# Two stages of mixture-of-experts behind graph attention: routing by chunks, slot lists from one-hot products, experts that gather their rows

## The chip, the cores and the metric

One Trainium2 chip, of which the program uses one core. The metric is the device time of one execution in microseconds (us), the median over the runs.

## The reference

A graph with N = 6250 nodes of D = 256 float32 features and E = 206250 edges goes through two layers. Each is graph attention and then a mixture of experts, both added to the residual:

```python
x = x + _L0_gnn_ref(_layernorm(x), ..., edge_attr_3, edge_index)
x = x + _L0_ffn_ref(_layernorm(x)[None], ...)[0]
x = x + _L1_gnn_ref(_layernorm(x), edge_index, ...)
x = x + _L1_ffn_ref(_layernorm(x)[None], ...)[0]
```

The two mixtures have 8 experts with 1024 hidden units. Layer 0's sends each token to its two best experts; before the experts it normalises its input a second time, with a scale and shift of each expert:

```python
probs = softmax(xt @ Wr + br); top_p, top_idx = top_k(probs, 2)
weights = top_p / top_p.sum(-1)
xn = (xt - mu) * rsqrt(var + 1e-5);  xe = xn * ln_g[e] + ln_b[e]
y = gelu(xe @ W1[e] + b1[e]) @ W2[e] + b2[e]
out = sum of weights * y over the two
```

Layer 1's sends each token to its best expert, drops what is over an expert's capacity (977 tokens), uses relu, multiplies by the probability, and replaces what is not finite.

## The kernel before

`build` (L1777) runs its stages one after the other, each with its own buffers and semaphores; between two stages all engines meet. They are: a plan of the edges; then for each layer a node stage (projections), an edge stage (attention, with rows gathered by GpSimd), and `ffn_phases` (L1216), which is a routing stage and an expert stage. The change is in `ffn_phases` and in one scratch tensor of `scratch`.

**Routing.** The tokens are NT = 49 tiles of 128, taken as 7 chunks of R = 7. SyncE loads a chunk's residual rows `r_xs` and attention sums `r_ag`, two chunks ahead, and stores the combined rows (`keep_rows`, L1289). VectorE combines each chunk (L1424 to L1436): it divides the sums by the denominators, seven multiplies of a tile each, every one waiting for the last (`done`), adds bias and residual, and takes the statistics. Only after the last chunk come mean and variance of all tiles (`stats`), the normalisation of 49 tiles (L1455), in layer 0 the statistics of the normalised rows (L1462) and a second normalisation (L1473). In one loop VectorE copies a tile to `r_xg` (L1468), TensorE transposes it (L1363), ScalarE copies it out (L1396) and TensorE multiplies it by the router's weights (L1369). Then VectorE works out softmax, choices, and by two matmuls (L1382, L1383) the place of each token among those of its expert. Experts' slots are laid out in blocks of TB = 256. SyncE has filled `sc_xb` with zeros meanwhile (L1312). GpSimd scatters each tile's rows, 258 numbers with token number and weight behind the features, to their slots in `sc_xb`: 49 indirect DMAs for the first choice (L1341), in layer 0 49 more for the second (L1347), each chunk of these behind VectorE's exchange of the weight in the row (L1560).

**Experts.** A loop over pairs of blocks, two buffers. SyncE's queue, for each block: its rows `x_xin` from `sc_xb` (L1606), in layer 0 scale and shift (L1608, L1609), both weight matrices of 1 MB, both biases (L1610 to L1613), all of them once VectorE has taken the outputs of the block before the last. TensorE: 16 fp32 matmuls into `x_ps_h` (L1676), the next block's four transposes (`turn`, L1661), 16 matmuls into `x_ps_y` (L1687). ScalarE applies the activation. VectorE makes `x_xT` of the next block (L1707 or L1710), adds the bias (L1738), weighs (L1744, L1748), in layer 1 bounds the values (L1752 to L1757) and adds the residual (L1761), and works out row numbers and weights of the next block from the last two columns of its rows (L1715 to L1720, `rows_of`). GpSimd's queue, in its order: in layer 1 two gathers of residual rows `x_xr` (L1641) as soon as those numbers are there; once the block is added, two scatters, in layer 0 accumulating (L1646), in layer 1 plain (L1649); a wait until they have landed. `hold` is a wait on a semaphore against a value of the loop.

## Time and profile before

| | |
|---|---|
| median of 3 runs | 6622.04 us (6620.52 to 6622.79) |
| the profiled execution | 6616.8 us |
| its span on the core | 6614.6 us |
| busy: TensorE, VectorE, ScalarE, GpSimd | 69%, 53%, 21%, 55% |
| granted TensorE clock, mean | 0.87 of 2.4 GHz |
| layer 0's routing stage | about 2474 to 2828 us |
| layer 0's expert stage | about 2828 to 3676 us |
| layer 1's routing stage | about 5897 to 6158 us |
| layer 1's expert stage | about 6158 us to the end |

Every stage is visible in the page's second part, which cuts the span into 40 slices. A record of TensorE is a half of an fp32 matmul. PE is TensorE, PEld its weight loads, DVE VectorE, ACT ScalarE, POOL GpSimd, SP SyncE; SPq and POOLq are DMA issues or the sequencer. A bracket behind a row tells how long the engine had been idle and what released it.

### The profile page before, as it was taken

Reading aid. Unit: us, or ns where it says so; the run is one execution under the profiler, and the core shown is the slowest. Engines: PE = TensorE matmul, PEld = TensorE weight load, DVE = VectorE, ACT = ScalarE, POOL = GpSimd, SP = SyncE. Lnnn points to the kernel's source line nnn. Section 1 sums busy time; section 2 is a strip of 40 time slices with the busy share of each in tenths; the row PEclk is TensorE's granted clock in tenths of the full one; section 3 lists DMA queues with packets and bytes.
Section 4 is the critical chain, followed back from the end, with each engine's and each line's share of the span. In section 5 each row is a group of like instructions: output and inputs, shape, how many; then the busy total and the mean of one; then the engine's idle time right before and its main releaser. Section 6 shows DMA issues by size and latency. Waiting matters only on the chain. (4 is left out here: it accounts for less than half of the span.)

```text
span 6614.6 us, 94515 instructions
## 1 busy us (share of the span) xinstructions
PE 4549.3 (69%) x18923; PEld 3390.2 (51%) x18923; DVE 3515.0 (53%) x6341; ACT 1391.7 (21%) x2978; POOL 3661.8 (55%) x3707
## 2 busy tenths in 40 slices
PE   1578888888888872189999435665656565643698
PEld 0345555555545552179999424444444444433698
DVE  5678787887878857111111334444444453544244
ACT  1333333333333320022222201111111111101122
POOL 1577777777777730512222177777777777711322
PEclk9899999999999995589999768888888888875899
DMA  7555555555555525255556555555555555532455
GB/s 215 176 164 162 159 165 157 165 161 158 162 159 162 160 74 211 74 169 184 184 184 184 137 137 138 142 137 142 138 141 139 140 141 138 141 108 110 171 199 187
DMA packets 717825, 1021.19 MB, mean 154 GB/s; under 512 B 301952, under 2 KB 531459, under 8 KB 692504
## 3 DMA queue, kind: packets, MB, share of 16 engines
q0 software_dynamic: 183456, 485.95, 27.8%
q1 hardware_dynamic: 488947, 491.67, 23.9%
q10 hardware_dynamic: 45188, 41.42, 2.0%
q14 instruction: 205, 1.67, 0.1%
q8 instruction: 29, 0.48, 0.0%
HBM read 868.25 MB, written 152.93 MB: 154 GB/s over the span
## 5 line engine op out<-in xcount | busy, mean ns | idle before, releaser
L767 POOL DMA_INDIRECT e_rows<-sc_table,e_eidx x3224 | 3164.9, 982 | 1019.4 <-issue 952.4
L872 PE MATMUL e_ps_o<-e_rows,e_oh 128*128 128x264 f32 x6448 | 1687.5, 407 | 154.6 <-ACT e_res L957 134.0
L872 PEld LDWEIGHTS e_ps_o<-e_rows,e_oh 128*128 128x128 f32 x6448 | 1211.5, 198 | 568.0 <-issue 389.9
L1132 DVE TENSOR_TENSOR e_rows<-e_rows,e_ps_w 128x1024 f32<-128x1024 f32 x806 | 970.4, 1207 | 11.0 <-ACT e_rows L953 10.9
L957 ACT COPY e_res<-e_ps_o 32x264 f32<-32x264 f32 x806 | 296.2, 368 | 1938.9 <-PE e_ps_o L876 1378.5
L844 PE MATMUL e_ps_X<-e_ident,e_alog 128*104 128x128 f32 x496 | 112.4, 399 | 811.5 <-ACT e_alog L937 811.5
L1062 DVE SCALAR_TENSOR_TENSOR e_u<-e_encr,e_adst,e_ps_hd 128x512 f32<-128x512 f32 x806 | 580.5, 739 | 162.9 <-ACT e_encr L933 106.5
L1676 PE MATMUL x_ps_h<-x_xT,x_w 128*128 128x256 f32 x2624 | 645.8, 404 | 14.8 <-DMA x_b<-in_L_ffn_b_dram 14.8
L1676 PEld LDWEIGHTS x_ps_h<-x_xT,x_w 128*128 128x128 f32 x2624 | 637.3, 337 | 18.8 <-issue 15.6
L1687 PE MATMUL x_ps_y<-x_w,x_hT 128*128 128x256 f32 x2624 | 579.9, 379 | 0.0
L933 ACT ACTIVATE e_encr<-e_ps_enc 128x512 f32<-128x512 f32 x806 | 477.3, 592 | 437.1 <-PE e_ps_enc L804 433.8
L1646 POOL DMA_INDIRECT sc_x<-x_y,x_idx x108 | 167.9, 1554 | 664.7 <-DVE x_idx L1720 648.1
L1687 PEld LDWEIGHTS x_ps_y<-x_w,x_hT 128*128 128x128 f32 x2624 | 492.9, 190 | 63.5
L844 PEld LDWEIGHTS e_ps_X<-e_ident,e_alog 128*104 128x104 f32 x496 | 95.1, 264 | 838.2 <-issue 838.2
L1085 DVE TENSOR_TENSOR e_ps_k<-e_ps_X,e_y 104x512 f32<-104x512 f32 x31 | 21.7, 699 | 845.5 <-ACT e_y L941 845.5
L1699 ACT ACTIVATE x_hT<-x_ps_h,x_b 128x256 f32<-128x256 f32 x656 | 305.1, 474 | 779.1 <-PE x_ps_h L1676 778.8
L876 PE MATMUL e_ps_o<-e_res,e_sel 128*128 128x264 f32 x1488 | 455.6, 388 | 0.0
L815 PE MATMUL e_ps_X<-e_u,e_hwide 128*104 128x512 f32 x806 | 416.2, 597 | 50.9 <-DVE e_u L1065 50.9
L804 PE MATMUL e_ps_enc<-e_at,e_w_enc 96*128 96x512 bf16 x806 | 309.2, 384 | 200.3 <-DVE e_u L1062 111.3
L1053 DVE TENSOR_SCALAR e_ohT<-e_at,e_nid 96x512 bf16<-96x512 int16 x806 | 295.3, 367 | 280.2 <-PE e_ps_X L820 210.8
L804 PEld LDWEIGHTS e_ps_enc<-e_at,e_w_enc 96*128 96x128 bf16 x806 | 78.0, 97 | 515.3 <-issue 506.6
L1341 POOL DMA_INDIRECT sc_xb<-r_xt,r_slot_i x98 | 94.7, 967 | 437.8 <-DVEq L1546 408.5
(291 smaller groups left out, 4402.3 us busy)
## 6 DMA issues: line engine op xcount, KB each, us to landing
x_w<-in_L_ffn_W_dram SPq DMA_DIRECT2D x112, 1024.0 KB
e_at<-sc_grp SPq DMA_DIRECT2D x403, 192.0 KB
x_w<-in_L_ffn_w_dram SPq DMA_DIRECT2D x60, 1024.0 KB
e_rows<-sc_table,e_eidx POOLq DMA_INDIRECT x3224
e_at<-sc_grp SPq DMA_DIRECT2D x403, 96.0 KB
sc_agg<-e_res ACTq DMA_DIRECT2D x806, 33.0 KB
...
```

What stands on the lines that cost most here:

```text
L767: pool.indirect_dma_start(rows[:, k, s, j, :], None, dr["table"][:, :], bass.IndirectOffsetOnAxis(eidx[:, k, s, j:j + 1], 0)).then_inc(s_r ...
L804: nc.tensor.matmul(ps_enc[:, :], w_enc[:, h * P:(h + 1) * P], at[:, ring(s), 0, :].bitcast(BF16), start=True, stop=True).then_inc(s_enc, 1)
L815: nc.tensor.matmul(ps_X[0:COLS, :], hwide[:, 0, COLS - HEADS * (s + 1):2 * COLS - HEADS * (s + 1)], u[:, par(s), 0, :], start=(s == 0), st ...
L872: nc.tensor.matmul(ps_o[:, 0:ROW], oh[:, k, at_j:at_j + P], rows[:, k, s, j, :], start=(j == 0), stop=False)
L876: nc.tensor.matmul(ps_o[:, 0:ROW], sel[:, k, s * WIN:s * WIN + P], seen, start=False, stop=True).then_inc(s_o, 1)
L933: nc.scalar.activation(encr[:, h, :], ps_enc[:, :], ACT.Relu).then_inc(s_relu, 1)
L957: nc.scalar.copy(res[0:WIN, kept(s), :], ps_o[0:WIN, 0:ROW]).then_inc(s_ev, 1)
L1062: nc.vector.scalar_tensor_tensor(u[:, p, h, :], encr[:, h, :], adst[:, h:h + 1], ps_hd[:, h, :], ALU.add, ALU.mult).then_inc(s_u, 1)
L1132: nc.vector.tensor_tensor(part, part, ps_w[:, k, :, s * HEADS:(s + 1) * HEADS].unsqueeze(3).to_broadcast([P, CH, HEADS, DH]), ALU.mult).th ...
L1676: mm = nc.tensor.matmul(ps_h[:, j % 4, 0:TB], w1[:, k, c, :].rearrange("p (m j) -> p j m", j=FC)[:, j, :], xT[:, k, c, :], start=(c == 0), ...
L1687: mm = nc.tensor.matmul(ps_y[:, s, 0:D], hT[:, k, j, s * P:(s + 1) * P], w2[:, k, j, :], start=(j == 0), stop=(j == FC - 1))
L1699: nc.scalar.activation(hT[:, k, j, :], ps_h[:, j % 4, 0:TB], ACT.Gelu if first else ACT.Relu, bias=b1[:, k, j:j + 1]).then_inc(s_act, 1)
```

## The change

In the routing stage, mean and variance of a chunk are worked out as soon as it is combined. ScalarE normalises it from scale and bias per row (`even`), which in layer 0 is the double normalisation at once; the logits are multiplied by the second standard deviation afterwards. TensorE transposes these rows directly, tile by tile, without the copy. SyncE stores the normalised rows in token order in `xn`, and the tokens' weights behind them, 2 numbers each. No rows are scattered and nothing is filled with zeros. Instead a list of slots is made: with a slot's number as 128 * hi + lo, VectorE makes for each tile and choice a one-hot row of lo (128 columns) and one of hi times a mark (120 columns in layer 0, 72 in layer 1), and TensorE's products of the two add up to a table of which token (and which choice) lies in each slot. In the expert stage GpSimd gathers a block's rows from `xn` by that list, while the block two before is in work; SyncE no longer loads rows, and issues the first weight matrix first. In layer 0 the weight of a row is chosen from its two by the list.

The diff, cut (new buffers, semaphores and GpSimd's constants left out):

```diff
+    def even_rows(c):
+        sp.wait_ge(s_xtn, (c + 1) * R)
+        sp.dma_start(xn[c * R * P:(c + 1) * R * P, 0:D].rearrange("(t p) d -> p t d", p=P),
+                     xt[:, c * R:(c + 1) * R, :]).then_inc(s_rows, 16)
...
+        if c >= 4:
+            even_rows(c - 4)
     for c in range(R - 2, R):
         sp.wait_ge(s_agu, c + 1)
         keep_rows(c)
     sp.dma_start(rows_in[NP:NP + TB, :].rearrange("(p s) d -> p (s d)", p=P), zero[:, 0:SUB * D]).then_inc(s_kept, 16)
-    sp.wait_ge(s_fill, 16 * -(-n_slot // (8 * P)))
-    sp.sem_inc(s_in, 1)
+    sp.dma_start(xn[NP:NP + TB, :].rearrange("(p s) d -> p (s d)", p=P), zero[:, :]).then_inc(s_rows, 16)
+    for c in range(R - 4, R):
+        even_rows(c)
+    sp.wait_ge(s_wq, 1)
+    with nc.allow_non_contiguous_dma(reason="a token's weights behind its row, once"):
+        sp.dma_start(xn[0:NP, D:XW].rearrange("(t p) d -> p t d", p=P), wgt[:, :, :]).then_inc(s_rows, 16)
     sp.wait_ge(s_kept, 16 * (R + 1))
+    sp.wait_ge(s_rows, 16 * (R + 2))
...
-    pool.wait_ge(s_in, 1)
-    pool.wait_ge(s_slot, 1)
-    for t in range(NT):
-        pool.indirect_dma_start(xb[:, :], bass.IndirectOffsetOnAxis(slot_i[:, 0, t:t + 1], 0),
-                                xt[:, t, :], None).then_inc(s_top[t // R], 16)
-    if first:
-        for t in range(NT):
-            if t % R == 0:
-                pool.wait_ge(s_w1, t // R + 1)
-            pool.indirect_dma_start(xb[:, :], bass.IndirectOffsetOnAxis(slot_i[:, 1, t:t + 1], 0),
-                                    xt[:, t, :], None).then_inc(s_sc, 16)
-        pool.wait_ge(s_sc, 16 * NT)
-    else:
-        for c in range(R):
-            pool.wait_ge(s_top[c], 16 * R)
...
+    def turn(t):
+        pe.wait_ge(s_xtn, t + 1)
+        if t >= 3:
+            pe.wait_ge(s_xT, t - 2)
         for c in range(DC):
+            mm = nc.tensor.transpose(ps_x[:, t % 3, c * P:(c + 1) * P], xt[:, t, c * P:(c + 1) * P], ident[:, :])
         mm.then_inc(s_t, 1)
+    def logits(t):
+        pe.wait_ge(s_xT, t + 1)
         for c in range(DC):
+            mm = nc.tensor.matmul(ps_l[:, t, :], xT[:, t % R, c, :], wr[:, c, :], start=(c == 0), stop=(c == DC - 1))
         mm.then_inc(s_l, 1)
+    for t in range(NT):
+        turn(t)
+        if t >= 2:
+            logits(t - 2)
+    logits(NT - 2)
+    logits(NT - 1)
...
+    for n in range(top * NT):
+        pe.wait_ge(s_ohl, n + 1)
+        pe.wait_ge(s_ohh, n + 1)
+        nc.tensor.matmul(ps_t[:, 0:n_hi], ohl[:, n % (2 * R), :], ohh[:, n % (2 * R), :],
+                         start=(n == 0), stop=(n == top * NT - 1)).then_inc(s_inv, 1)
...
+    def even(c):
+        act.wait_ge(s_nb, c + 1)
+        for t in range(c * R, (c + 1) * R):
+            nc.scalar.activation(xt[:, t, :], xs[:, t, :], ACT.Identity, bias=nb[:, t:t + 1], scale=rstd[:, t:t + 1]).then_inc(s_xtn, 1)
+            if t >= 2:
+                copy(t - 2)
+    def copy(t):
+        act.wait_ge(s_t, t + 1)
+        if t >= R:
+            act.wait_ge(s_l, t - R + 1)
+        nc.scalar.copy(xT[:, t % R, :, :], ps_x[:, t % 3, 0:D].rearrange("p (c n) -> p c n", c=DC)).then_inc(s_xT, 1)
+    act.wait_ge(s_zero, 3)
+    for c in range(R):
+        act.wait_ge(s_var, c + 1)
+        if first:
+            nc.scalar.activation(std[:, :, c * R:(c + 1) * R], var[:, c, :, :], ACT.Sqrt, bias=eps[:, 0:1]).then_inc(s_std, 1)
+        else:
+            nc.scalar.activation(std[:, 0, c * R:(c + 1) * R], var[:, c, 0, :], ACT.Sqrt, bias=eps[:, 0:1]).then_inc(s_std, 1)
+        if c >= 1:
+            even(c - 1)
+    even(R - 1)
+    copy(NT - 2)
+    copy(NT - 1)
...
+    def whole(o, i, m, a):
+        ts(o, i, m, a, ALU.mult, ALU.add)
+        ts(o, o, 12582912.0, None, ALU.add)
+        ts(o, o, -12582912.0, None, ALU.add)
...
+    def combine(c):
         v.wait_ge(s_x[c], 32 if first and c == R - 1 else 16)
         v.wait_ge(s_ag[c % 2], 16 * (c // 2 + 1))
+        tiles = slice(c * R, (c + 1) * R)
+        rows = xs[:, tiles, :]
         sums, dens = ag[:, c % 2, :, 0:D], ag[:, c % 2, :, D:ROW]
         ts(dens, dens, 1e-10, None, ALU.max)
         done(nc.vector.reciprocal(dens, dens))
+        tt(rows, rows, bias[:, :].unsqueeze(1).to_broadcast([P, R, D]), ALU.add)
         for r in range(R):
+            ins = nc.vector.tensor_tensor(ag[:, c % 2, r, 0:D].rearrange("p (h c) -> p h c", h=HEADS),
+                                          ag[:, c % 2, r, 0:D].rearrange("p (h c) -> p h c", h=HEADS),
+                                          ag[:, c % 2, r, D:ROW].unsqueeze(2).to_broadcast([P, HEADS, DH]), ALU.mult)
+        done(ins)
         tt(rows, rows, sums, ALU.add)
         v.sem_inc(s_agu, 1)
         for t in range(c * R, (c + 1) * R):
             nc.vector.bn_stats(st[:, t, :], xs[:, t, :]).then_inc(s_stat, 1)
+        v.wait_ge(s_stat, (c + 1) * R)
+        m, d = mean[:, tiles], dif[:, :]
+        tt(m, st[:, tiles, 1], st[:, tiles, 4], ALU.add)
         ts(m, m, 0.5, None, ALU.mult)
+        tt(d, st[:, tiles, 1], st[:, tiles, 4], ALU.subtract)
         done(nc.vector.scalar_tensor_tensor(d, d, 0.25, d, ALU.mult, ALU.mult))
+        tt(var[:, c, 0, :], st[:, tiles, 2], st[:, tiles, 5], ALU.add)
+        done(nc.vector.scalar_tensor_tensor(var[:, c, 0, :], var[:, c, 0, :], 1.0 / D, d, ALU.mult, ALU.add))
+        if first:
+            ts(d, var[:, c, 0, :], EPS, None, ALU.add)
+            done(nc.vector.reciprocal(d, d))
+            tt(var[:, c, 1, :], var[:, c, 0, :], d, ALU.mult)
         v.sem_inc(s_var, 1)
+    def finish(c):
+        tiles = slice(c * R, (c + 1) * R)
+        v.wait_ge(s_std, c + 1)
         if first:
+            tt(rstd[:, tiles], std[:, 0, tiles], std[:, 1, tiles], ALU.mult)
+            done(nc.vector.reciprocal(rstd[:, tiles], rstd[:, tiles]))
+        else:
+            done(nc.vector.reciprocal(rstd[:, tiles], std[:, 0, tiles]))
+        done(nc.vector.scalar_tensor_tensor(nb[:, tiles], mean[:, tiles], -1.0, rstd[:, tiles], ALU.mult, ALU.mult))
+        v.sem_inc(s_nb, 1)
+    for c in range(R):
+        combine(c)
+        if c >= 1:
+            finish(c - 1)
+    finish(R - 1)
...
+    if first:
+        tt(lg[:, :, :], ps_l[:, 0:NT, :], wide(std[:, 1, :]), ALU.mult)
+        tt(lg[:, :, :], lg[:, :, :], each(br[:, :]), ALU.add)
+    else:
+        tt(lg[:, :, :], ps_l[:, 0:NT, :], each(br[:, :]), ALU.add)
...
+        whole(hi[:, c, :], c1[:, 7, :], 1.0 / P, 0.5 / P - 0.5)
+        done(nc.vector.scalar_tensor_tensor(lo[:, c, :], hi[:, c, :], -float(P), c1[:, 7, :], ALU.mult, ALU.add))
+        for t in range(NT):
+            n = c * NT + t
+            if n >= 2 * R:
+                v.wait_ge(s_inv, n - 2 * R + 1)
+            nc.vector.tensor_scalar(ohh[:, n % (2 * R), :], iotah[:, :], hi[:, c, t:t + 1], mark[:, c, t:t + 1],
+                                    ALU.is_equal, ALU.mult).then_inc(s_ohh, 1)
+            nc.vector.tensor_scalar(ohl[:, n % (2 * R), :], iotap[:, :], lo[:, c, t:t + 1], None, ALU.is_equal).then_inc(s_ohl, 1)
...
+    v.wait_ge(s_inv, top * NT)
+    done(nc.vector.tensor_copy(held[:, 0, :], ps_t[:, 0:n_hi]))
     if first:
+        whole(held[:, 1, :], held[:, 0, :], 0.5, -0.25)
+        done(nc.vector.scalar_tensor_tensor(choice[:, :, 1], held[:, 1, :], -2.0, held[:, 0, :], ALU.mult, ALU.add))
+        ts(choice[:, :, 0], choice[:, :, 1], -1.0, 1.0, ALU.mult, ALU.add)
+    else:
+        done(nc.vector.tensor_copy(held[:, 1, :], held[:, 0, :]))
+    done(nc.vector.scalar_tensor_tensor(held[:, 2, :], held[:, 1, :], 0.0, spare[:, :, :].rearrange("p b s -> p (b s)"),
+                                        ALU.is_equal, ALU.mult))
+    done(nc.vector.scalar_tensor_tensor(held[:, 3, :], held[:, 1, :], -1.0, held[:, 2, :], ALU.add, ALU.add))
+    done(nc.vector.tensor_copy(token[:, :], held[:, 3, :]))
...
-        sp.dma_start(xin[:, k, :, :], xb[bass.ds(b * TB, TB), :].rearrange("(s p) d -> p s d", p=P)).then_inc(s_ldx[k], 16)
+        sp.dma_start(w1[:, k, :, :], one(names["w1"]).rearrange("a (p c) f -> (a p) c f", c=DC)).then_inc(s_ldw[k], 16)
         if first:
             sp.dma_start(lng[:, k, :], one("L0_ffn_ln_g").rearrange("a (p c) -> (a p) c", c=DC)).then_inc(s_ldx[k], 16)
             sp.dma_start(lnb[:, k, :], one("L0_ffn_ln_b").rearrange("a (p c) -> (a p) c", c=DC)).then_inc(s_ldx[k], 16)
-        sp.dma_start(w1[:, k, :, :], one(names["w1"]).rearrange("a (p c) f -> (a p) c f", c=DC)).then_inc(s_ldw[k], 16)
...
+    def gather(k):
+        for s in range(SUB):
+            pool.indirect_dma_start(xin[:, k, s, :], None, xn[:, :],
+                                    bass.IndirectOffsetOnAxis(take[:, k, s:s + 1], 0)).then_inc(s_gx[k], 16)
+    for k in range(2):
+        pool.wait_ge(s_ix, k + 1)
+        gather(k)
...
+            hold(pool, s_ix, i * 2 + (k + 3), s_pq)
+            hold(pool, s_wt, i * 2 + (k + 1), s_pq)
+            gather(k)
+            hold(pool, s_give, i * 2 + (k + 1), s_pq)
             if not first:
                 for s in range(SUB):
                     pool.indirect_dma_start(xr[:, k, s, :], None, rows_in[:, :],
-                                            bass.IndirectOffsetOnAxis(idx[:, k, s:s + 1], 0)).then_inc(s_gx[k], 16)
+                                            bass.IndirectOffsetOnAxis(give[:, k, s:s + 1], 0)).then_inc(s_xr[k], 16)
...
-            hold(pe, s_ldx[1 - k], (i + k) * n_ldx + n_ldx, s_pp)
+            hold(pe, s_gx[1 - k], (i + k) * n_sc + n_sc, s_pp)
+            if first:
+                hold(pe, s_ldx[1 - k], (i + k) * n_ldx + n_ldx, s_pp)
...
             hold(v, s_t, i * 2 + (k + 2), s_pv)
             affine(1 - k)
+            hold(v, s_gx[k], i * n_sc + n_sc, s_pv)
+            nc.vector.tensor_copy(take[:, k, :], token[:, bass.ds((i * 2 + (k + 2)) * SUB, SUB)]).then_inc(s_ix, 1)
+            if first:
+                nc.vector.tensor_tensor(wc[:, k, :, :], xin[:, k, :, D:XW], choice[:, bass.ds((i * 2 + k) * SUB, SUB), :],
+                                        ALU.mult).then_inc(s_wc, 1)
+                hold(v, s_wc, i * 2 + (k + 1), s_pv)
+                nc.vector.tensor_reduce(wt[:, k, :], wc[:, k, :, :], AX_X, ALU.add).then_inc(s_wt, 1)
+            else:
+                nc.vector.tensor_copy(wt[:, k, :], xin[:, k, :, D]).then_inc(s_wt, 1)
+            hold(v, s_free, i * 2 + (k + 1), s_pv)
+            nc.vector.tensor_copy(give[:, k, :], token[:, bass.ds((i * 2 + k) * SUB, SUB)]).then_inc(s_give, 1)
             hold(v, s_y, i * 2 + (k + 1), s_pv)
-            hold(v, s_free, i * 2 + (k + 1), s_pv)
...
-            hold(v, s_free, i * 2 + (k + 2), s_pv)
-            rows_of(1 - k, i * 8 + (4 * k + 4))
```

## Rows read from the trace of the kernel before

**Rows 1.** Busy time by engine (x records), clock, DMA share, GB/s

```profile
2518.50:2529.00 10.50, 0.00 (x0) 0.00 (x0) 10.01 (x19) 0.00 (x0) 0.00 (x0) 0.50 0.86 265
2600.00:2661.00 61.00, 59.34 (x285) 55.70 (x285) 29.84 (x97) 17.95 (x49) 0.00 (x0) 0.50 0.00 0
2842.00:3650.00 808.00, 808.00 (x3646) 762.74 (x3646) 151.23 (x532) 233.59 (x459) 164.75 (x106) 1.00 0.59 182
```

**Rows 2.** Timeline, routing of layer 0: start, duration, engine, operation, [idle]

```profile
2486.84 0.19 DVE L1414 TENSOR_SCALAR r_ag<-r_ag 128x56 f32<-128x56 f32 x1 [10.62 <-DMA r_br<-in_L_ffn_br_dram]
...
2487.61 3.18 DVE L1411 TENSOR_TENSOR r_ag<-r_ag 128x256 f32<-128x256 f32 x7
...
2497.36 0.17 DVE L1414 TENSOR_SCALAR r_ag<-r_ag 128x56 f32<-128x56 f32 x1
...
2621.72 0.48 PEld L1363 LDWEIGHTS r_ps_x<-r_ident,r_xg 128*128 128x128 f32 x2
...
2622.90 0.48 PEld L1363 LDWEIGHTS r_ps_x<-r_ident,r_xg 128*128 128x128 f32 x2
...
2663.19 0.57 DVE L1411 TENSOR_TENSOR r_lg<-r_ps_l,r_br 128x392 f32<-128x392 f32 x1 [8.20 <-PE r_ps_l L1369]
...
2679.65 0.57 DVE L1514 COPY r_tot<-r_ps_c 128x392 f32<-128x392 f32 x1 [3.13 <-PE r_ps_c L1383]
...
2692.22 0.11 DVE L1548 MEMSET r_trow<- 1x64 f32 x1 [0.18 <-DVE r_xt L1545]
...
2828.47 0.20 POOL L1628 MEMSET x_ident<- 128x128 f32 x1 [10.69 <-POOLq L59]
...
2841.14 9.48 PE L1676 MATMUL x_ps_h<-x_xT,x_w 128*128 128x256 f32 x32 [7.62 <-DMA x_b<-in_L_ffn_b_dram]
```

**Rows 3.** Timeline, routing of layer 1

```profile
5909.48 0.19 DVE L1414 TENSOR_SCALAR r_ag<-r_ag 128x56 f32<-128x56 f32 x1 [9.73 <-DMA r_br<-in_L_ffn_gate_b_dram]
...
6066.33 0.57 DVE L1411 TENSOR_TENSOR r_lg<-r_ps_l,r_br 128x392 f32<-128x392 f32 x1 [10.74 <-PE r_ps_l L1369]
...
6077.36 0.57 DVE L1514 COPY r_tot<-r_ps_c 128x392 f32<-128x392 f32 x1 [3.13 <-PE r_ps_c L1383]
...
6157.93 0.20 POOL L1628 MEMSET x_ident<- 128x128 f32 x1 [6.79 <-POOLq L59]
```

**Rows 4.** Groups of VectorE by shape: busy us, mean ns | idle before

```profile
L1455 DVE TENSOR_SCALAR r_xt<-r_xs,r_lnv x98 | 32.9, 408 | 1.6 <-DVE r_lnv L1449 1.0
...
L1748 DVE TENSOR_SCALAR x_y<-x_y,x_wt 128x256 f32<-128x256 f32 x56 | 17.2, 350 | 9.5 <-DVE x_y L1738 9.5
...
L492 DVE TENSOR_SCALAR n_amat<-n_amask,n_avec 128x8 f32<-128x8 f32 x8 | 1.9, 231 | 7.2 <-DMA n_avec<-in_L_gnn_attn_r_dram 3.9 <-DMA n_avec<-in_L_gnn_a_dst_dram 3.1
...
L1414 DVE TENSOR_SCALAR r_e<-r_e 128x8 f32<-128x8 f32 x8 | 1.4, 172 | 0.3
```

**Rows 5.** Timeline, edge stage of layer 1: last gather of a batch, first reader

```profile
3848.20 0.94 POOL L767 DMA_INDIRECT e_rows<-sc_table,e_eidx  x1 [0.30 <-issue]
...
3851.09 0.54 ACT L937 COPY e_alog<-e_rows 128x416 f32<-128x416 f32 x1 [87.97 <-DMA e_rows<-sc_table,e_eidx]
```

**Rows 6.** Timeline of SyncE's queue at the end of layer 1's node stage

```profile
3765.74 0.39 SPq L374 DMA_DIRECT2D sc_a2p<-n_a2p  x1
3776.85 0.30 SPq L662 DMA_DIRECT2D e_nbi<-sc_nblk  x1
```

**Rows 7.** Timeline, expert stage of layer 1, one block

```profile
6343.50 0.69 DVE L1761 TENSOR_TENSOR x_y<-x_y,x_xr 128x512 f32<-128x512 f32 x1 [0.34 <-DVE x_y L1757]
...
6345.11 1.02 POOL L1649 DMA_INDIRECT out_dram<-x_y,x_idx  x1 [7.96 <-DVE x_y L1761]
...
6349.92 0.99 POOL L1641 DMA_INDIRECT x_xr<-sc_x,x_idx  x1 [2.48 <-issue]
...
6359.45 0.63 PE L1661 MATMUL x_ps_x<-x_ident,x_xin 128*128 128x128 f32 x4
```

More of the change, by code:

```diff
@@ L1232, in ffn_phases @@
         cnt_i = keep("cnt_i", [1, 4], I32)
+        token = keep("token", [P, n_hi], I32)
+        choice = keep("choice", [P, n_hi, 2], F32)
         with ExitStack() as ctx:
@@ L1272, in ffn_phases @@
             ps_c = ps("ps_c", [P, 2, 512])
+            ps_t = ps("ps_t", [P, 512])
             s_x = [sem(f"x{c}") for c in range(R)]
             s_ag = [sem(f"ag{c}") for c in range(2)]
-            s_w, s_const, s_zero, s_fill, s_sum, s_chain, s_stat, s_var, s_std, s_agu, s_xtn = (
-                sem(n) for n in ("w", "const", "zero", "fill", "sum", "chain", "stat", "var", "std", "agu", "xtn"))
-            s_xg, s_t, s_xT, s_l, s_lg, s_pick, s_cnt, s_slot, s_sc, s_pp, s_pa, s_pv, s_soft, s_exp, s_in = (
-                sem(n) for n in ("xg", "t", "xT", "l", "lg", "pick", "cnt", "slot", "sc", "pp", "pa", "pv", "soft", "exp", "in"))
-            s_kept, s_w1 = sem("kept"), sem("w1")
-            s_top = [sem(f"top{c}") for c in range(R)]
-            pslot = lambda k: k % 2 if k < R - 1 else 2
+            s_w, s_const, s_zero, s_chain, s_stat, s_var, s_std, s_nb, s_agu, s_xtn = (
+                sem(n) for n in ("w", "const", "zero", "chain", "stat", "var", "std", "nb", "agu", "xtn"))
+            s_t, s_xT, s_l, s_pick, s_cnt, s_soft, s_exp, s_wq, s_slot, s_ohl, s_ohh, s_inv, s_kept, s_rows = (
+                sem(n) for n in ("t", "xT", "l", "pick", "cnt", "soft", "exp", "wq", "slot", "ohl", "ohh", "inv", "kept", "rows"))
             block = ctx.enter_context(nc.Block())
@@ L1370, in logits @@
                     mm.then_inc(s_l, 1)
-                with pe.Fori(0, NT // R) as i:
-                    turn(i, 0)
-                    turn(i, 1)
-                    for k in range(R):
-                        if k + 2 < R:
-                            turn(i, k + 2)
-                        logits(i, k)
+                for t in range(NT):
[4 more added lines that the diff above has]
+                logits(NT - 1)
@@ L1388, in _ @@
-                nc.scalar.activation(lnv[:, 3, :], lnv[:, 1, :], ACT.Sqrt, bias=eps[:, 0:1]).then_inc(s_std, 1)
-                if first:
-                    act.wait_ge(s_var, 2)
-                    nc.scalar.activation(lnv[:, 3, :], lnv[:, 1, :], ACT.Sqrt, bias=eps[:, 0:1]).then_inc(s_std, 1)
-                act.sem_inc(s_xT, 2)
-                with act.Fori(0, NT // R) as i:
-                    for k in range(R):
-                        hold(act, s_t, i * R + (k + R + 1), s_pa)
-                        nc.scalar.copy(xT[:, k, :, :], ps_x[:, pslot(k), 0:D].rearrange("p (c n) -> p c n", c=DC)).then_inc(s_xT, 1)
+                def even(c):
[4 more added lines that the diff above has]
+                            copy(t - 2)
@@ L1567, in ffn_phases @@
             xin = sb("xin", [P, 2, SUB, XW], F32)
+            xr = sb("xr", [P, 2, SUB, D], F32)
             w1 = sb("w1", [P, 2, DC, FF], F32)
@@ L1652, in _ @@
                         pool.sem_inc(s_free, 1)
+                for k in range(2):
+                    hold(pool, s_gx[k], pairs * n_sc + n_sc, s_pq)
             @block.tensor
```

185 lines of the change are left out of this document (72 added, 113 removed).

## The prediction

> **What bounds the kernel now.** I began with the page's second part: twice TensorE is idle or at its lower clock while VectorE or GpSimd works alone, before each expert stage. The windows then say what each stretch is. In layer 0's expert stage TensorE is busy for all of 808 us at full clock: 3646 records, 0.222 us each; a block has 68 (two per fp32 matmul), so 15.07 us a block [rows 1]. Nothing that the change does beside TensorE there can gain. The routing stage is a chain instead. In the timeline read where each link starts: in layer 0 VectorE combines from 2486.84, 10.52 us a chunk; TensorE's tile loop ends just before the softmax at 2663.19; the counts come back at 2679.65; the slots are ready at 2692.22; then GpSimd scatters alone, and the experts' stage starts at 2828.47 [rows 2]. That is 342 us, 136 of them after the slots. In layer 1 it is 5909.48 to 6157.93, 248 us [rows 3]. So the change is priced as two shorter chains, plus what the expert stages may lose.
>
> **Combining (L1424 to L1475).** Seven chained multiplies took 3.18 us a chunk [rows 2]. Unchained they cost about their 256 columns, 0.35 each as the nearest 256-column operation [rows 4], 2.5 us: minus 0.65. Each chunk gets its own statistics, six small operations, in layer 0 three more for the second variance, then two or three for scale and bias. A small operation takes 0.172 [rows 4] and about 0.03 to the next, a reciprocal a little more. Layer 0: 12 at 0.205 = 2.5, so 10.52 - 0.65 + 2.5 = 12.4 us; layer 1: 8, so 11.5. Seven chunks: 86.8 and 80.5. Gone are both whole passes over the rows and the copies into `r_xg`; ScalarE normalises instead.
>
> **Transposes and logits.** A tile costs TensorE 1.18 us, the distance of two tiles [rows 2]. ScalarE now has a copy and a normalisation per tile; a copy is 0.37 (17.95 us for 49, [rows 1]), two are 0.74, so TensorE sets the tile. Seven tiles, 8.3 us, fit under a chunk of VectorE. The last two chunks do not: the normalisation of the sixth is queued on ScalarE behind the square root of the seventh, so 14 tiles, 16.5 us, remain, plus some 2 us to fill and drain. Softmax in layer 0: 2486.84 + 86.8 - 0.7 + 18.5 = 2591.4 instead of 2663.2. Layer 1: 5909.5 + 80.5 - 0.5 + 18.5 = 6008.0 instead of 6066.3.
> These tiles run at the lower level: over 61 us TensorE was busy 97% and the granted clock stayed at 0.50, 1.2 GHz [rows 1]. The Trainium skill ("TensorE: Matmul & The Clock Gate", Part 1) says that a TensorE kept busy is given its full clock; the row does not agree, and I go by the row. By the rule the sum would be some 6360 instead of 6377.
>
> **From softmax to token lists.** Softmax to counts was 16.46 us [rows 2]; plus 0.6 for the square root put back into the logits, minus 0.2 for `r_valid`, minus 1.2 for the weights, which now lie under the 3.13 us wait for the counts: 15.6. Counts to slots was 12.57; the two address rounds stay, seven small operations again each, and the two writes into `r_xt` go: 12.0. Layer 1: 6077.36 - 6066.33 = 11.0, less 0.2 [rows 3]; then 12.0 less one round (2.8), with the four operations on the capacity that layer 0 has not (1.6): 10.8.
> New are the one-hots, two VectorE operations a tile and choice, 98 pairs in layer 0 and 49 in layer 1. The trace has none of this shape. With one column as scalar, 8 columns cost 0.231 and 256 cost 0.350, so 0.00048 a column; a second scalar column adds 0.058 (0.408, [rows 4]). That gives 0.289 for 128 columns and 0.343 for 120; back to back they come some 0.04 to 0.06 closer: 0.53 a pair, 0.50 in layer 1 with 72 columns. Bounds: 0.40, two small operations; 0.76, two at 256 columns. I take 0.53, interpolated between rows of the same operation: 51.5 and 24.5 us. TensorE's matmul of a pair is hidden if shorter: 256 columns take 2 x 0.222 us at full clock, 0.89 at half, and 120 of 256 columns 0.42. Its upper bound is 0.89, unscaled: then TensorE sets the pair.
> Behind the one-hots come the table of blocks (14 small operations, 3.7 us, which waited for nobody before) and the lists (9 and 5 operations: 2.5 and 1.3). Sums: 15.6 + 12.0 + 51.5 + 3.7 + 2.5 = 85.3 us; layer 1: 10.8 + 10.8 + 24.5 + 3.4 + 1.3 = 50.8.
>
> **Leaving the stage.** Between the last scatter and the experts' first instruction lay 10.69 us in layer 0 [rows 2] and 6.79 in layer 1 [rows 3], landing included. Landing alone took about 2.0 behind a gather (3848.20 + 0.94 to 3851.09, [rows 5]), so retiring the semaphores and meeting takes 4.8 at most and 0 at least; now everything has landed, and I take 3. Layer 0's experts start at 2591.4 + 85.3 + 3 = 2679.7, not 2828.47: 148.8 us less. Layer 1: 6008.0 + 50.8 + 3 = 6061.8, not 6157.93: 96.1 less.
>
> **DMAs moved and added.** The 15 and 9 zero fills and 147 scatters go. SyncE gets seven stores of normalised rows, each behind a wait for its chunk; three lie among the loads. Behind those waits are the next chunk's loads, asked for a chunk early. A chunk with all four transfers moves 3.6 MB; the stretch of before moved 265 GB/s at a share of 0.86, so 308 at most, 11.7 us [rows 1]: under 12.4, beside 11.5. Cost 0 to 10 us, I take 0, since only three chunks a layer are so full. The weights are 6272 pieces of 8 bytes; a store of as many pieces of 48 bytes was issued at 3765.74 and the next stage's first DMA followed at 3776.85, so 11.1 us at most [rows 6]. It hides under the one-hots, 24.5 us and more; without them it would be 11 a layer.
>
> **Expert stages.** Taking the rows' load off SyncE's queue and starting with four gathers changes the 12.7 us to the first matmul [rows 2] little, since that waits for the weights and biases: -1 to +2, I take 0. On GpSimd each block gets two gathers, ahead of the block's own work, so its scatter is queued behind them. In layer 1: scatter at 6345.11, residual gather at 6349.92 [rows 7]. The new gathers take that place, 2.6 us; the residual ones end 2.3 later at 6354.8 and land 2.0 after that [rows 5], at 6356.8. VectorE wants them a block after 6343.50, at 6358.6. Slack 1.8 us: no cost. The new gathers land by 6354.1 and are needed at 6359.45. Layer 0 has no residual gather and more slack. VectorE's four or five list operations replace four. They stand in mid-block, behind two waits: for the block's own gather, and for the scatter of two blocks before. Queued behind them is the addition that frees the accumulator TensorE needs next; that scatter has landed by 6349.92, half a block before the same point, so nothing is paid.
>
> **Sum.** 148.8 + 96.1 = 245 us off the profiled 6616.8 (6614.6 of span and 2.2 around it), which lies 5.2 below the median of the runs; off the median 6622.0 it gives 6377.
>
> **Rivals.**
> *TensorE sets the one-hot pairs.* At 0.89 the pairs take 87 and 44 us: 35.5 and 19.5 more, 6432. For it: weight loads at the lower clock. Against: they were hidden in every block. 0.05.
> *The clock rises in the routing.* TensorE would step to 2.4 GHz in the tile loop: the last 14 tiles take half as long at best, 8.3 us less a layer: 6360. Against it stand the 61 us at 0.50 [rows 1]. (It is the Trainium skill's rule named above.) 0.04.
> *The stores make the combining DMA-bound.* At 265 GB/s a full chunk takes 13.6 us: 1.2 and 2.1 over, three times each: plus 10, 6387. 0.06.
> *GpSimd's chain becomes layer 1's bound,* so that the gather a block and a half ahead is not what it says but a new wait. If the residual gather lands over 1.8 us later, VectorE's addition slips, and with it the next scatter. At 4.0 us more: 2.2 us in 28 blocks (56 multiplies, two each, [rows 4]): plus 62, 6439. 0.04.
> *Slower: the row gathers stall the experts.* Needed once a block on GpSimd's queue, they have 5.3 us to spare in layer 1. Losing 245 us in some 82 blocks takes 3.0 us each, so a gather pair of over 12.5 us instead of 4.2. At 14 us: 82 x 4.5 = 369, so 6746. Against: the edge stage's gathers land 2.0 us after issue. 0.02.
>
> **How the numbers follow.** The forecast's own mechanism has 0.79. Its range: the pair at 0.40 gives -19, at 0.76 +35; small operations per chunk and leaving +/-10; DMA +10. With rivals at both ends 6345 to 6425 holds 8 in 10; TensorE or GpSimd as a full bound lie beyond it. A change of 0.2%, 13 us, is what this kernel's measurement can tell. Faster by more 0.97, within 0.01, slower 0.02.
>
> **What would show it.** Experts start near 2679; a chunk of 12.4 us and 11.5; softmax 18 us behind the last chunk; pairs at 0.53 and 0.50, VectorE without waits for TensorE; expert blocks still at 15.07 with TensorE never waiting for a row gather. Pairs paced by TensorE, granted clock 1.0 in the routing, or idle TensorE in blocks of layer 1 would prove me wrong.

## The result and the profile after

The changed kernel takes 6421.9 us (median of 4 runs, 6420.1 to 6423.5), the kernel before 6622.2 beside it: a ratio of 0.970 (95% interval 0.9687 to 0.9713), 200 us less. The forecast was 245 less. The profiled span went from 6614.6 to 6420.9.

The timeline of the routing in layer 0 after the change (start, duration, engine, line, operation, [idle before]) answers to [rows 2]:

```profile
2488.33 0.19 DVE L1450 TENSOR_SCALAR r_ag<-r_ag 128x56 f32<-128x56 f32 x1 [9.60 <-DMA r_br<-in_L_ffn_br_dram]
...
2595.43 0.57 DVE L1447 TENSOR_TENSOR r_lg<-r_ps_l,r_std 128x392 f32<-128x392 f32 x1 [18.07 <-PE r_ps_l L1385]
...
2611.03 0.57 DVE L1557 COPY r_tot<-r_ps_c 128x392 f32<-128x392 f32 x1 [1.77 <-PE r_ps_c L1398]
...
2619.02 0.34 DVE L1590 TENSOR_SCALAR r_ohh<-r_iotah,r_hi,r_mark 128x120 f32<-128x120 f32 x1
...
2665.72 0.11 DVE L1594 MEMSET r_trow<- 1x64 f32 x1
...
2669.20 0.28 DVE L1605 COPY r_held<-r_ps_t 128x120 f32<-128x120 f32 x1
...
2673.02 0.24 DVE L1786 COPY x_take<-f_token 128x2 int32<-128x2 int32 x2 [1.29 <-PEq L59]
```

And layer 1, answering to [rows 3]:

```profile
5767.88 0.19 DVE L1450 TENSOR_SCALAR r_ag<-r_ag 128x56 f32<-128x56 f32 x1 [9.51 <-DMA r_br<-in_L_ffn_gate_b_dram]
...
5869.23 0.57 DVE L1447 TENSOR_TENSOR r_lg<-r_ps_l,r_br 128x392 f32<-128x392 f32 x1 [18.27 <-PE r_ps_l L1385]
...
5880.04 0.57 DVE L1557 COPY r_tot<-r_ps_c 128x392 f32<-128x392 f32 x1 [3.13 <-PE r_ps_c L1398]
...
5889.82 0.32 DVE L1590 TENSOR_SCALAR r_ohh<-r_iotah,r_hi,r_mark 128x72 f32<-128x72 f32 x1
...
5910.56 0.09 DVE L1594 MEMSET r_trow<- 1x40 f32 x1
...
5916.60 0.24 DVE L1786 COPY x_take<-f_token 128x2 int32<-128x2 int32 x2 [1.52 <-PEq L59]
```

From the first chunk to the experts' first instruction layer 0 now takes 184.7 us (before 341.6), layer 1 148.7 (before 248.4): 256.7 us gained, 12 more than forecast. So the shortfall lies elsewhere, and a ledger of the stages finds it. From the experts' start to the addition behind the last block's second matmuls, layer 0 went from 827.4 us (2828.47 to 3655.89) to 839.3 (2673.02 to 3512.29): 11.9 lost. Layer 1, experts' start to the end of the span, went from 456.7 to 504.3: 47.6 lost. All that lies between adds 3.5: layer 0's first chunk starts 1.5 later, and from that last addition to layer 1's first chunk it takes 2.0 longer. The sum is -193.7, the difference of the spans.

The windows (width, then busy us and records of TensorE's matmuls, its weight loads, VectorE, ScalarE and GpSimd, granted clock, DMA share, GB/s) of combining, tile loop, two stretches of one-hots in layer 0, one in layer 1, and both expert stages; they answer to [rows 1]:

```profile
2501.00:2564.00 63.00, 32.08 (x160) 31.39 (x160) 57.81 (x149) 24.88 (x62) 0.00 (x0) 0.50 0.82 251
2578.00:2595.00 17.00, 17.00 (x88) 17.00 (x88) 0.00 (x0) 12.23 (x27) 0.00 (x0) 0.50 0.58 172
...
2619.00:2629.00 10.00, 9.38 (x42) 7.62 (x42) 9.98 (x45) 0.00 (x0) 0.00 (x0) 0.76 0.00 0
...
2649.00:2664.00 15.00, 15.00 (x68) 9.96 (x68) 15.00 (x69) 0.00 (x0) 0.00 (x0) 1.00 0.01 1
...
5900.00:5910.00 10.00, 10.00 (x49) 10.00 (x49) 10.00 (x49) 0.00 (x0) 0.00 (x0) 0.50 0.00 0
...
2690.00:3505.00 815.00, 810.30 (x3628) 759.82 (x3628) 150.22 (x530) 231.12 (x456) 276.08 (x212) 1.00 0.62 178
5950.00:6400.00 450.00, 413.79 (x1815) 384.51 (x1814) 175.95 (x428) 100.14 (x212) 172.60 (x160) 0.98 0.48 177
```

A block has 68 records, so in layer 0 it now takes 815 / 3628 x 68 = 15.28 us, where [rows 1] gave 15.07; in layer 1 it takes 16.9. There TensorE is idle for 36 of 450 us and its clock is under 1.00. The waits of that stage (engine, tile, line <- what ended the wait: us in total, times, longest):

```profile
POOL out_dram L1715 <- DVE x_y L1830: 177.3, 28, 8.1
...
DVE x_y L1830 <- DMA x_xr<-sc_x,x_give: 121.8, 26, 5.9
POOL x_xin L1687 <- issue: 87.0, 54, 3.4
...
PE x_ps_x L1729 <- DMA x_xin<-sc_xn,x_take: 34.0, 19, 3.1
```

Two of these are new: VectorE's last addition waits for the residual in 26 blocks (in [rows 7] it followed the bounds at once), and TensorE waits for gathered rows in 19. One block, timeline:

```profile
6139.02 0.69 DVE L1830 TENSOR_TENSOR x_y<-x_y,x_xr 128x512 f32<-128x512 f32 x1 [5.20 <-DMA x_xr<-sc_x,x_give]
...
6140.63 1.02 POOL L1715 DMA_INDIRECT out_dram<-x_y,x_give  x1 [6.03 <-DVE x_y L1830]
6141.95 1.01 POOL L1715 DMA_INDIRECT out_dram<-x_y,x_give  x1 [0.30 <-issue]
...
6145.73 0.99 POOL L1687 DMA_INDIRECT x_xin<-sc_xn,x_take  x1 [2.77 <-issue]
...
6146.75 0.34 SPq L1663 DMA_DIRECT2D x_w<-in_L_ffn_w_dram  x1
...
6147.02 1.49 POOL L1687 DMA_INDIRECT x_xin<-sc_xn,x_take  x1 [0.30 <-issue]
...
6148.81 1.20 POOL L1707 DMA_INDIRECT x_xr<-sc_x,x_give  x1 [0.30 <-issue]
...
6150.32 1.46 POOL L1707 DMA_INDIRECT x_xr<-sc_x,x_give  x1 [0.30 <-issue]
...
6154.23 0.72 PE L1729 MATMUL x_ps_x<-x_ident,x_xin 128*128 128x128 f32 x4 [1.61 <-DMA x_xin<-sc_xn,x_take]
...
6155.83 0.69 DVE L1830 TENSOR_TENSOR x_y<-x_y,x_xr 128x512 f32<-128x512 f32 x1 [4.83 <-DMA x_xr<-sc_x,x_give]
```

Addition to addition is a closed cycle of 16.81 us: 1.6 from the addition's start to the first scatter, 2.3 for both scatters, 2.8 until they have landed, 6.05 for four gathers, 4.05 until the residual is there. The weights' loads (2 MB a block) are issued at 6146.75, into the middle of the gathers; the three behind it take 1.2 to 1.5 us to issue instead of 0.95, and the landing takes twice the 2.0 of [rows 5]. It isn't the worst block: over the 27 distances between additions the four gathers take 5.5 us on average, and the residual is there 4.7 us behind the last of them (3.1 to 6.3). "A block and a half ahead" has become 4 us ahead: the rows issued by 6148.51 are needed at 6152.6. The same thing shows at the stage's first long block, by windows:

```profile
5977.00:5984.00 7.00, 5.65 (x24) 5.35 (x23) 3.49 (x6) 3.31 (x7) 5.04 (x4) 1.00 0.86 328
5984.00:5991.00 7.00, 5.69 (x20) 4.83 (x21) 1.57 (x6) 0.00 (x0) 2.02 (x2) 0.76 0.29 95
```

While gathers and weights run together the DMA engines are at a share of 0.86, 328 GB/s; TensorE then waits 2.67 us for its rows, and the granted clock falls to a mean of 0.76, so that the block's second matmuls (32 records) take 8.75 us instead of 7.07. Layer 1's 27 block distances, taken from where VectorE adds the bias: 8 at 15.05, 15 at 15.9 to 17.4, 4 at 19.0 to 21.2, together 46.5 us above 27 x 15.05. The clock fell in 4 of the 19 blocks that had waited for rows, and their second matmuls took 7.5 us more in all; so most of the loss is the waiting itself.

Layer 0's loss has other waits, those ahead of TensorE's transposes:

```profile
PEld x_ps_x L1729 <- issue: 12.1, 29, 1.1
PE x_ps_x L1729 <- DMA x_lnb<-in_L_ffn_ln_b_dram: 4.2, 14, 0.8
```

And the transposes of one block, in the timeline:

```profile
3014.19 0.72 PE L1729 MATMUL x_ps_x<-x_ident,x_xin 128*128 128x128 f32 x4 [0.21 <-DMA x_lnb<-in_L_ffn_ln_b_dram]
```

What TensorE waits for is not a gather but 1 KB of norm shift. When the row load left SyncE's queue, the change also moved the first weight matrix ahead of the norm vectors (L1663 before L1665), so each of them queues behind 1 MB.

### The profile page after: what moved, and what is told of

It reads as the page before. It is cut to its first block and busy times, and to the rows that moved or that the text cites. A ratio compares the mean times of both kernels' runs of the same rounds, so it can differ in the third digit from the quotient of the medians.

```text
span 6420.9 us, 94121 instructions
## 1 busy us (share of the span) xinstructions
PE 4640.7 (72%) x19217; PEld 3458.7 (54%) x19217; DVE 3487.1 (54%) x6434; ACT 1438.6 (22%) x3087; POOL 3716.1 (58%) x3742
## 5 line engine op out<-in xcount | busy, mean ns | idle before, releaser
L1687 POOL DMA_INDIRECT x_xin<-sc_xn,x_take x172 | 175.4, 1020 | 890.1 <-issue 503.1
L876 PEld LDWEIGHTS e_ps_o<-e_res,e_sel 128*128 128x128 f32 x1488 | 289.5, 195 | 51.4
```

Source lines behind the costliest of these rows:

```text
L876: nc.tensor.matmul(ps_o[:, 0:ROW], sel[:, k, s * WIN:s * WIN + P], seen, start=False, stop=True).then_inc(s_o, 1)
```

## The experiments

Ratios are to the kernel before, run beside each; times are the ratio times 6622.2. Theory A: the cycle through GpSimd and VectorE sets layer 1's block. Rivals: the rows land late wherever they stand (B), landing is slow without any load (A2). For layer 0, theory C is the order of SyncE's loads.

**Wait for the landing after the gathers** (layer 1; at the start two more gathers into a free tile give the first wait its count).

```diff
                         hold(pool, s_give, ...)
                         ...                       # two residual gathers
+                        if not first:
+                            hold(pool, s_sc[1 - k], i * n_sc + n_sc, s_pq)
+                            pool.sem_inc(s_free, 1)
                         hold(pool, s_add, i * 2 + (k + 1), s_pq)
                         ...                       # two scatters
-                        hold(pool, s_sc[k], i * n_sc + n_sc, s_pq)
-                        pool.sem_inc(s_free, 1)
```

> Layer 1 only: GpSimd waits for a scatter's landing after the next block's gathers and not ahead of them. Theory A (the cycle scatter, landing, two row gathers, two residual gathers, their landing, VectorE's addition, next scatter is what sets layer 1's block): 2.7 us leave a cycle of 16.8, so 14.1, under TensorE's 15.05: the block returns to 15.05, layer 1's expert stage from 504.3 to about 457, total about 6375. Theory B (TensorE waits for the rows because the DMA engines are loaded with the weights, wherever the gathers stand): block stays near 16.8, total about 6420. In between (15.5 a block, 6390) would say that the landing grows as the wait goes.

Ratio 0.9625 (0.961 to 0.964), so 6374. All 27 block distances are 15.05. In its timeline the gathers follow the scatters at once:

```profile
6253.23 1.00 POOL L1722 DMA_INDIRECT out_dram<-x_y,x_give  x1 [0.31 <-DVE x_take L1809]
6254.53 0.99 POOL L1687 DMA_INDIRECT x_xin<-sc_xn,x_take  x1 [0.30 <-issue]
...
6258.35 0.95 POOL L1711 DMA_INDIRECT x_xr<-sc_x,x_give  x1 [0.30 <-issue]
...
6260.92 0.34 SPq L1663 DMA_DIRECT2D x_w<-in_L_ffn_w_dram  x1
...
6265.32 0.69 DVE L1840 TENSOR_TENSOR x_y<-x_y,x_xr 128x512 f32<-128x512 f32 x1 [0.26 <-DVE x_y L1836]
```

The last gather is issued before the weights are asked for, each takes 0.95 to 0.99, and the addition waits for nothing. Theory A holds; B, by which the block would have stayed at 16.8, does not.

**The residual gathers first** (layer 1; the two pairs of gathers change places on GpSimd).

```diff
+                        ...                       # give, two residual gathers
                         hold(pool, s_ix, i * 2 + (k + 3), s_pq)
                         hold(pool, s_wt, i * 2 + (k + 1), s_pq)
                         gather(k)
-                        ...                       # give, two residual gathers
```

> Layer 1 only: the two residual gathers stand ahead of the two row gathers in GpSimd's program. Theory A: the row gathers (2.8 us with the gap) leave the cycle, 16.8 to 14.0, VectorE's addition no longer waits for the residual; but the rows for TensorE are then asked for 2.7 us later in the block and may be late for its transposes by up to 1.5 us: a block of 15.05 to 16.0, total 6375 to 6402. Theory B: the rows are what TensorE waits for, so asking for them later makes the block longer than 16.8: total 6450 or more.

Ratio 0.9649 (0.9634 to 0.9663): 6390. Every second block takes 15.05, most others 15.4 to 16.6 and one 20.0; the mean is 15.68. Now the addition is on time, and what is left is the other coupling, rows asked for too late in the block:

```profile
6262.04 0.69 DVE L1834 TENSOR_TENSOR x_y<-x_y,x_xr 128x512 f32<-128x512 f32 x1 [0.26 <-DVE x_y L1830]
...
6264.17 0.72 PE L1733 MATMUL x_ps_x<-x_ident,x_xin 128*128 128x128 f32 x4 [0.73 <-DMA x_xin<-sc_xn,x_take]
```

**Norm vectors ahead of the first weights** (layer 0).

```diff
-                    sp.dma_start(w1[:, k, :, :], ...)
                     if first:
                         sp.dma_start(lng[:, k, :], ...)
                         sp.dma_start(lnb[:, k, :], ...)
+                    sp.dma_start(w1[:, k, :, :], ...)
```

> Layer 0 only: SyncE asks for the two norm vectors ahead of the first weight matrix, as before the change, and not behind it. Theory C (layer 0's block went from 15.07 to 15.28 because TensorE's transposes wait for two small vectors that queue behind 1 MB of weights): the 0.2 us return in 54 blocks, about 11 us, total about 6410. Rival D (it is the row gathers that land late, or their traffic): no change, total 6421 within 2.

Ratio 0.9681 (0.9668 to 0.9694): 6411. The interval overlaps that of the changed kernel (0.9687 to 0.9713), so the stage has to tell: experts' start to last addition takes 828.8 us (2671.20 to 3500.01), 10.5 less than after the change, and TensorE is never idle in it:

```profile
2690.00:3490.00 800.00, 800.00 (x3616) 755.55 (x3615) 150.03 (x530) 229.89 (x453) 275.15 (x212) 1.00 0.60 180
```

Theory C holds. The gathers cost layer 0 at most the 1.4 us that are left.

**Two more gathers a block in the kernel before** (layer 1, ahead of the residual gathers, into a tile nobody reads).

```diff
+                            for s in range(SUB):
+                                pool.indirect_dma_start(more[:, k, s, :], None, rows_in[:, :],
+                                                        bass.IndirectOffsetOnAxis(idx[:, k, s:s + 1], 0)).then_inc(s_more[k], 16)
                             for s in range(SUB):
                                 pool.indirect_dma_start(xr[:, k, s, :], ...
```

> The kernel before the change with two more gathers on GpSimd in each block of layer 1, ahead of the residual gathers, into a tile that nobody reads. Theory A: the cycle on GpSimd alone is enough: the addition waits for the residual, blocks of 16 to 17 us, total 6622 + 30 to 50 = 6650 to 6670. Theory B: nothing reads the new rows and TensorE's rows come from SyncE's queue, so it costs under 5 us: 6622 to 6627.

Ratio 1.0016 (1.0006 to 1.0025): 11 us, between the two expectations, neither of which was right. The cycle is there, VectorE waits for the residual in 25 blocks:

```profile
DVE x_y L1768 <- DMA x_xr<-sc_x,x_idx: 148.3, 25, 8.1
```

but its blocks take 15.43 us on average, 10 us in all. The cycle itself is shorter here. From the fifth distance between additions on it is 15.4 on average: 1.6, 2.4 and 2.7 up to the scatters' landing, as before, then 5.3 for four gathers and 3.4 until the residual is there. What differs is where the weights' loads fall:

```profile
6376.52 0.33 SPq L1612 DMA_DIRECT2D x_w<-in_L_ffn_w_dram  x1
...
6377.47 1.04 POOL L1643 DMA_INDIRECT x_more<-sc_x,x_idx  x1 [2.46 <-issue]
```

Here they are issued ahead of the first gather in 24 of 27 blocks, in the changed kernel behind it in 24 of 27. They are released when VectorE takes the block's outputs. In the changed kernel that comes late when TensorE has waited for gathered rows; in the kernel before its rows come on SyncE's queue. That this second coupling lengthens the cycle from 15.4 to 16.9 us fits the rows but is argued: no run moves the weights' loads alone.

**Small weights** (layer 1's loop loads 16 elements per partition of each matrix).

```diff
-                    sp.dma_start(w1[:, k, :, :], one(names["w1"])...)
+                    sp.dma_start(w1[:, k, 0, 0:16], one(names["w1"])...[:, 0, 0:16])
                     ...                           # w2 likewise
```

> The changed kernel, except that layer 1's loop loads 16 of each partition's elements of both weight matrices instead of all: this leaves the weights of later blocks out of the computation, while the number of transfers and of waits stays. Theory A1 (the cycle is over 15.05 only because gathers and residual land beside 2 MB of weights): residual lands about 2.0 us behind its issue instead of 4, cycle about 13.5, every block 15.05, total 6422 - 48 = 6374. Theory A2 (landing takes 4 us whatever runs beside it): cycle 15.5 or more, blocks 15.5 to 17, total 6385 to 6420.

Ratio 0.9629 (0.9614 to 0.9644): 6377; TensorE's 27 block distances are all 15.05. The order on GpSimd is that of the changed kernel and the landing is still waited for, but 100 of the 108 gathers are issued in 0.95 to 1.0 us (in the changed kernel 53), and VectorE waits for the residual in only 4 blocks, 3.5 us in all. A block as most are:

```profile
6142.10 0.95 POOL L1713 DMA_INDIRECT x_xr<-sc_x,x_give  x1 [0.30 <-issue]
...
6146.60 0.69 DVE L1836 TENSOR_TENSOR x_y<-x_y,x_xr 128x512 f32<-128x512 f32 x1 [0.26 <-DVE x_y L1832]
```

A1 holds: the cycle is too long only beside the weights' traffic. It is close to the limit even so, since the additions come 14.6 to 16.0 us apart.

**No residual gathers** (layer 1).

```diff
-                                pool.indirect_dma_start(xr[:, k, s, :], ...).then_inc(s_xr[k], 16)
-                            hold(v, s_xr[k], i * n_sc + n_sc, s_pv)
+                nc.vector.memset(xr[:, :, :, :], 0.0)      # once, at the start
```

> The changed kernel without the residual gathers of layer 1 (a tile of zeros is added in their place, so the residual is left out of the output). Theory A' (the residual's landing makes the addition late, that the scatter, that the row gathers, and these TensorE): without it the addition follows the bounds at once, the row gathers stand ahead of the weights' loads, every block 15.05, total 6422 - 48 = 6374. Rival (the row gathers are late on their own, behind the scatter's landing and beside the weights): blocks stay over 15.3, total 6385 or more.

Ratio 0.9626 (0.9609 to 0.9643): 6374, all distances 15.05. The row gathers stand where they stood, behind the scatter's landing, and are in time. Standing there, they are late only when the addition is.

**The sixth chunk's tiles early** (both layers).

```diff
                 for c in range(R):
+                    if c == R - 1:
+                        finish(c - 1)
                     combine(c)
-                    if c >= 1:
+                    if 1 <= c < R - 1:
                         finish(c - 1)
```

(and on ScalarE `even(c - 1)` ahead of the last square root)

> The changed kernel; scale and bias of the sixth chunk are made, and its tiles normalised, ahead of the seventh chunk's combining, in both layers. Theory E (14 tiles at TensorE's 1.18 us are left behind the last chunk because the sixth is queued behind the seventh's square root): seven of them, 8.3 us, go under the seventh chunk, against up to 1 us that VectorE waits for the square root: 7 to 8 us less in each layer, total about 6406. Rival F (the tail is latency of the last tiles, not their number): under 3 us in each layer, 6416 to 6422.

Ratio 0.969 (0.9677 to 0.9703): 6417. In its routing stages (first chunk to experts' start) layer 0 takes 180.2 us, layer 1 145.0, so 4.5 and 3.7 less: between E and F. The wait for the logits did fall by 6.6 us, but the last square root now stands on ScalarE behind the sixth chunk's tiles, and VectorE waits for it:

```profile
2575.40 0.17 DVE L1449 TENSOR_TENSOR r_rstd<-r_std 128x7 f32<-128x7 f32 x1 [2.30 <-ACT r_std L1427]
...
2587.78 0.57 DVE L1449 TENSOR_TENSOR r_lg<-r_ps_l,r_std 128x392 f32<-128x392 f32 x1 [11.44 <-PE r_ps_l L1385]
```

**What paces the one-hot pairs.** Two kernels, one run each (6433 and 6452 us, with one more matmul and with one more one-hot), so each is read by the stretch from the first one-hot to the memset behind the last and not by its time.

```diff
+                    nc.tensor.matmul(ps_x[:, 0, 0:n_hi], ohl[...], ohh[...], ...)
                     nc.tensor.matmul(ps_t[:, 0:n_hi], ohl[...], ohh[...], ...)
```

> The changed kernel with a second matmul of the same shape per one-hot pair, into a PSUM bank that nobody reads. It tells what TensorE needs for a pair. If VectorE alone paces the pairs (0.45 and 0.42 us) and TensorE has half its time free, the pair stays under 0.6 us, the stage at most 15 us longer in layer 0. If TensorE was at its limit beside VectorE, the pair doubles to 0.8 to 0.9: 35 to 44 us more in layer 0, 19 to 22 in layer 1.

```diff
+                        nc.vector.tensor_scalar(spareoh[:, n % (2 * R), :], iotap[:, :], lo[:, c, t:t + 1], None, ALU.is_equal)
                         nc.vector.tensor_scalar(ohl[:, n % (2 * R), :], iotap[:, :], lo[:, c, t:t + 1], None, ALU.is_equal)
```

> The changed kernel with a third one-hot of 128 columns per pair on VectorE, into a tile that nobody reads. If VectorE paces the pairs, each grows by what one operation takes in a row of them, 0.20 to 0.29: the pair to 0.65 to 0.74, 20 to 28 us more in layer 0, half of that in layer 1. If TensorE paces them, the pair stays within 0.1 of 0.45 and 0.42.

The third one-hot makes the stretch 66.0 us in layer 0 and 30.4 in layer 1 instead of 46.7 and 20.7: 0.197 a pair in both. VectorE is the pace-setter, and a one-hot beside others of its kind costs 0.20, though its row says 0.28. In layer 0 the granted clock now stays at 0.50 (window 2650 to 2665, TensorE busy 12.3 of 15 us), and VectorE sets the pace all the same. The second matmul leaves layer 0 at 46.8 us: there the clock is 1.00 and TensorE had half its time free. In layer 1 the clock stays at 0.50 all through, and TensorE paces the pairs: VectorE's 24 operations in 10 us are 12 pairs, 0.83 us each. VectorE may run 14 pairs ahead, so its own stretch grows only to 31.2 us; from the first one-hot to the experts' start it is 45.5 instead of 26.8.

```profile
2618.00:2628.00 10.00, 10.00 (x92) 10.00 (x92) 10.00 (x46) 0.00 (x0) 0.00 (x0) 1.00 0.01 2
...
5901.00:5911.00 10.00, 10.00 (x49) 10.00 (x49) 5.91 (x24) 0.00 (x0) 0.00 (x0) 0.50 0.00 0
```

Two matmuls in 0.83 are some 0.42 for one, and after the change a pair there takes 0.41 with TensorE busy 10 of 10 us: in layer 1 both engines are at their limit together, in layer 0 only VectorE.

**The edits together.** First those of the expert stages, then with the sixth chunk as well.

> The changed kernel with the edits of the expert stages alone (landing waited for behind the gathers, norm vectors ahead of the first weights). If both theories hold side by side, every block of both layers is at 15.05 to 15.07 and the total is the forecast's 6377 less the 12 us that the routing gained over the forecast: 6363 to 6367. If something else in the expert stages costs time, 6370 or more.

> The changed kernel with three edits together: the landing waited for behind the gathers (layer 1), the norm vectors ahead of the first weights (layer 0), the sixth chunk's tiles early (both). If the three gains add up: 48 + 11 + 15 below 6422, so 6348. If the shorter routing or the earlier gathers meet a new wait in the expert stages, 6355 or more.

Ratios 0.9601 (0.9588 to 0.9614), 6358, and 0.9591 (0.9577 to 0.9604), 6351; the sixth chunk's 7 us between the two lie within their intervals, but the routing stages of the two traces differ by 8.1. The first lies 5 us under what was expected, within its interval; the second, 3 above the plain sum of the gains, shows no new wait. TensorE is busy throughout both expert stages; the rows are those of the second:

```profile
2690.00:3490.00 800.00, 800.00 (x3618) 755.26 (x3617) 151.55 (x536) 228.93 (x451) 276.40 (x212) 1.00 0.61 183
5950.00:6330.00 380.00, 380.00 (x1720) 358.69 (x1720) 166.59 (x405) 95.61 (x202) 149.63 (x153) 1.00 0.56 199
```

With three edits the changed kernel gains 271 us over the kernel before instead of 200.

## Why the prediction was right or wrong

The sign and the two shorter chains were right. By the medians the forecast of 6377 was 45 us too low; by the spans it is 51, since the profiled execution of before lay 5 below its median and that of after 1 above. 60 us of loss in the expert stages and 3 in between, less 12 us of further gain in the routing, make up the 51.

The range, 6345 to 6425, holds the result by 3 us, and that was luck. It was meant to leave out GpSimd's chain as a bound of layer 1, which is what came. Without the 12 us by which the routing was better than forecast the time would have been about 6434.

*Combining.* A chunk was 12.6 us on average in layer 0 (six distances, 2488.33 to 2563.79; forecast 12.4) and 11.8 in layer 1 (11.5). VectorE never waited for a transfer behind the first chunk, although the DMA share was 0.82: the rival of the stores did not occur. A full chunk moves 3.7 MB and not 3.6, by the way (896 rows, three times 1 KB and once 1056 bytes), so at 265 GB/s it would have taken 14.0 us.

*Tail of tiles.* VectorE waited 18.1 and 18.3 us behind the last chunk, forecast 18.5, and the tile loop stayed at 0.50. The sixth chunk's experiment bears out that its tiles are part of that tail, by 6.6 us. From the first chunk to the softmax it took 107.1 and 101.4 us, forecast 104.6 and 98.5: both terms together were 5.4 us too small, hidden in the better total.

*Softmax to counts.* 15.6 and 10.8, as forecast.

*One-hots.* Counts to the end of the one-hots took 54.7 and 30.5 us, forecast 63.5 and 35.3. This is where the extra gain is: a pair is 0.44 (34 in the 15 us from 2649) and 0.41 (24.5 in the 10 us from 5900) instead of 0.53 and 0.50. The mechanism (VectorE paces, TensorE hidden) was right, the term was mis-sized. I took each operation's own duration less 0.05; neighbours overlap by about 0.09. The lower bound of 0.40 was nearer. (98 pairs at 0.53 are 51.9 us and not 51.5, and 0.40 would have given -18 and not -19.)

*TensorE sets the pairs (rival).* No: but in layer 1, at the lower clock, it needed 0.42, a hair from deciding. The rival's 0.89 was that of 256 columns, these are 72.

*The clock rises (rival).* Not in the tile loop, where it would have paid. It did rise under the one-hots of layer 0, to 0.76 and then 1.00, when TensorE's work there was a steady row of matmuls; in layer 1's it stayed at 0.50, with TensorE busy 10 of 10 us. The Trainium skill's rule ("TensorE: Matmul & The Clock Gate", Part 1) that a TensorE kept busy is given its full clock thus agrees with the one-hots of layer 0 and not with those of layer 1. Neither outcome changed the time, since VectorE needs some 0.4 us a pair in both.

*Leaving the stage.* 1.3 and 1.5 us, I took 3. The bound of 0 to 4.8 was right.

*Expert stages: the step that failed.* "Slack 1.8 us: no cost" put the cycle at 13.3 us a block: 1.6 to the scatter, 4.8 to the first gather, 4.9 for four gathers, 2.0 for the landing. It is 16.9 on average. The four gathers took 5.5, since some are issued more slowly beside the weights, and the way up to them 0.4 more. The largest part is the landing: it was taken from a gather of the edge stage, 2.0 us [rows 5], where no 2 MB of weights were on the way, and here it is 4.7. That is the rival "GpSimd's chain becomes layer 1's bound", to which I gave 0.04 on the strength of a duration from another stage. Its place was right. Its price (62) is near the measured 47.6, but for part of the reasons: it had no slower issue and no second path. The experiment on the kernel before shows that the same chain costs 10 us while TensorE's rows don't hang on it. In the changed kernel they do, by gathers which I had checked only against an undelayed schedule, and the clock falls in some of TensorE's waits.

Layer 0 was costed at nothing because it has no residual gather, which was right; what cost 11.9 there was a line of the diff that I read as the removal of a load and not as a new order of the rest.
